# A delta-rule attention and FFN block: half of the small matmuls turned to other columns of the array, and a 64x64 block-diagonal state

## What is computed

```python
def step(S, inp):                      # per head: S is 32x32
    qt, kt, vt, bt = inp
    v_pred = einsum('bhk,bhkv->bhv', kt, S)
    delta = (vt - v_pred) * bt[..., None]
    S = S + kt[..., None] * delta[:, :, None, :]
    ot = einsum('bhk,bhkv->bhv', qt, S)
...
q = xn @ Wq;  k = xn @ Wk;  v = silu(xn @ Wv);  beta = sigmoid(xn @ Wb)
o = delta_rule(l2norm(q) * 32**-0.5, l2norm(k), v, beta)
o = o * rsqrt(mean(o*o) + eps) * o_norm_weight;   attn = o @ Wo
ffn = down(silu(gate(xn)) * up(xn))
return x + attn + ffn
```

## Time and profile before

| | |
|---|---|
| runs, median (lowest to highest) | 2339.17 us (2338.87 to 2341.85) |
| the profiled execution | 2343.81 us |
| its span, first to last instruction | 2342.1 us |
| PE, DVE, ACT busy | 2235.0, 1786.9, 857.9 us |
| mean granted TensorE clock | 0.993 of full |

### The profile page before, as it was taken

One profiled execution on the slowest core, in us unless ns is written; L12 is line 12 of the kernel. 1 busy time (PEld: TensorE's weight loads), 2 busy tenths in 40 slices (PEclk: granted clock), 3 DMA queues, 4 the chain that ended last, 5 costly groups with the idle time before them and its releaser, 6 DMA issues.

```text
span 2342.1 us, 89426 instructions
## 1 busy us (share of the span) xinstructions
PE 2235.0 (95%) x40464; PEld 1228.6 (52%) x40688; DVE 1786.9 (76%) x3167; ACT 857.9 (37%) x2077; POOL 265.7 (11%) x519
## 2 busy tenths in 40 slices
PE   2899999999999999999999999999999999999996
PEld 1455555555546555455555546555455555546553
DVE  8986968778686786968768696786968768697775
ACT  4652524325242342523325242342423325242341
POOL 2101010020100101011020100101011020100100
PEclk9899999999999999999999999999999999999998
DMA  7000111101111001111001111001111001111000
GB/s 256 20 7 17 37 21 38 17 7 38 21 37 22 24 16 21 37 22 38 12 12 38 21 37 22 15 26 21 37 21 38 12 12 38 21 37 22 12 10 20
DMA packets 89978, 68.96 MB, mean 29 GB/s; under 512 B 68480, under 2 KB 68480, under 8 KB 89600
## 3 DMA queue, kind: packets, MB, share of 16 engines
q1 hardware_dynamic: 88880, 63.20, 9.6%
q10 hardware_dynamic: 720, 0.03, 0.0%
HBM read 30.72 MB, written 16.78 MB: 20 GB/s over the span
## 4 chain that ended last, share of the span: by engine, by line
PE 93%; DVE 4%; issue 2%; DMA 1%; ACT 0%; SPq 0%
PE D L440 28%; PE T L355 22%; PE D L430 22%; PE D L506 14%; PE D L371 7%; DMA qt<-in_L_attn_Wq_dram 1%; DVE outer_v L1198 1%; DVE at L1205 1%; DVE amax L935 0%; DVE kq L925 0%; DVE wd L926 0%; DVE wgu L926 0%; DVE f_hi L925 0%; DVE f_lo L925 0%; DVE qt L1383 0%
## 5 line engine op out<-in xcount | busy, mean ns | idle before, releaser
L440 PE MATMUL D<-xt,wgu 128*128 128x512 f16 x3072 | 689.6, 381 | 8.2 <-ACT sg L720 6.4
L430 PE MATMUL D<-xt,w_hi 128*128 128x512 f16 x1664 | 489.1, 380 | 24.4 <-DVE w_lo L978 24.4
L440 PEld LDWEIGHTS D<-xt,wgu 128*128 128x128 f16 x3072 | 291.9, 98 | 357.0 <-ACT sg L720 6.9
L430 PE MATMUL D<-xt,w_lo 128*128 128x512 f16 x768 | 291.9, 380 | 0.0
L1205 DVE TENSOR_TENSOR at<-at,outer_v 128x62 f32<-128x62 f32 (+15 forms) x496 | 262.2, 529 | 11.8
L1198 DVE TENSOR_TENSOR outer_v<-mt,at 128x62 f32<-128x62 f32 (+15 forms) x496 | 260.9, 526 | 13.0
L430 PEld LDWEIGHTS D<-xt,w_hi 128*128 128x128 f16 x1664 | 159.0, 98 | 212.7 <-issue 26.2
L506 PE MATMUL D<-wd,f_hi 128*128 128x512 bf16 x656 | 248.7, 379 | 17.8 <-issue 17.8
L506 PE MATMUL D<-wd,f_lo 128*128 128x512 bf16 x656 | 248.8, 379 | 16.1 <-issue 15.3
L710 ACT ACTIVATE kpv<-kpv,rk 128x32 f32<-128x32 f32 x1024 | 231.1, 307 | 1.5
L772 ACT ACTIVATE qt<-T 128x256 f32<-128x256 f32 x128 | 49.0, 383 | 465.4 <-DVE outer_p L1341 465.4
(11 more groups left out here) (173 smaller groups left out, 2597.5 us busy)
## 6 DMA issues: line engine op xcount, KB each, us to landing
xs<-_attn_hidden_states_dram SPq DMA_DIRECT2D x32, 512.0 KB, 3.5
out_dram<-xs SPq DMA_DIRECT2D x32, 512.0 KB, 3.0
fuse<-in_L_ffn_gate_w_dram SPq DMA_DIRECT2D x2, 768.0 KB, 8.3
xs<-in_L_ffn_up_w_dram SPq DMA_DIRECT2D x2, 768.0 KB, 9.1
f_hi<-in_L_ffn_down_w_dram SPq DMA_DIRECT2D x2, 768.0 KB, 10.1
f_lo<-in_L_ffn_down_w_dram SPq DMA_DIRECT2D x2, 768.0 KB, 11.7
kpv<-in_L_attn_Wk_dram SPq DMA_DIRECT2D x1, 1024.0 KB, 11.0
qt<-in_L_attn_Wq_dram SPq DMA_DIRECT2D x1, 1024.0 KB, 13.0
```

What stands on the lines that cost most here:

```text
L430: last = nc.tensor.matmul(D[bank][:, :], w[:, k, cols], xp[:, k, :], start=n == 0, stop=n == len(products) - 1)
L440: last = nc.tensor.matmul(D[bank][:, :], wgu[:, n // 2, c:c + P], (xt_hi, xt_lo)[n % 2][:, n // 2, :], start=n == 0, stop=n == 2 * KT_ - 1)
```

## The change

**Turned layout.** The batches are no longer alike. For batch 1 everything that lies by tokens (kt, vt, pt, the solution tt, beta) has its 64-partition halves swapped, so its matmuls go from strip h of the inputs to strip h^2 of the output: off the diagonal of the array, into the other bank of a pair. In all small stages the calls of batch 0 and batch 1 now alternate, quad by quad; before, 8 quads (or 4 in the chain) of one batch followed each other.

**Block state.** `state` gets two 32x32 slots per strip, one zero, so two heads stand on the diagonal of a 64x64 block. The prediction uses `pairs`: two 64x64 matmuls in place of a quad of four 32x32, 16 in place of 32 a step. DVE updates the state in two masked operations (`of_pair` is 0 or 1 by partition).

**Output.** Q S and P (U - W S) now lie in columns of their own (128 columns per group m instead of 96). ACT copies Q S, DVE adds the other (`add_inner`), one step later.

**Turning.** Reads that turn batch 1 are split in three, one over 128 partitions and two over 64: K transposes, beta's sum, the U copies, the output copies. V goes through ACT first (Silu from PSUM to `sg`), then DVE transposes. `V_AT` moves. `gram(2m)` and `gram(2m+1)` become one call with one semaphore at its end, as do the two U and W calls of a group.

```diff
-V_AT = {0: 0, 2: 1, 7: 2, 12: 3}
+V_AT = {0: 0, 4: 1, 8: 2, 13: 3}
...
+            def pairs(out, lhs, rhs, turned):
+                for h in range(2):
+                    s = slice(64 * h, 64 * h + 64)
+                    to = slice(64 * (1 - h), 64 * (1 - h) + 64) if turned else s
+                    last = nc.tensor.matmul(out[to], lhs[s], rhs[s], start=True, stop=True)
...
                 for h in range(QUADS):
                     s = slice(32 * h, 32 * h + 32)
-                    last = nc.tensor.matmul(out[s], lhs[s], rhs[s], start=start, stop=True, skip_group_check=shared)
+                    to = slice(32 * (h ^ 2), 32 * (h ^ 2) + 32) if turned else s
+                    last = nc.tensor.matmul(out[to], lhs[s], rhs[s], start=True, stop=True)
...
-                            pe.wait_ge(u_ready, since(8, g - 3))
+                            pe.wait_ge(u_ready, since(8, 2 * m - 2))
...
-                        for b in range(BATCH):
-                            for m in range(MS):
+                        for m in range(MS):
+                            for b in range(BATCH):
                                 pc = m * BC + b * STEPS + c
-                                last = quads(T[2 * (c % 2) + b][:, 96 * m:96 * m + 64], state[:, b, m, :],
-                                             kq_flat[:, 64 * pc:64 * pc + 64], start=m == 0, shared=True)
+                                last = pairs(T[2 * (c % 2) + b][:, 128 * m:128 * m + 64], state[:, b, m, :, :].rearrange("p e d -> p (e d)"),
+                                             kq_flat[:, 64 * pc:64 * pc + 64], b == 1)
...
-                        nc.scalar.activation(vt[:, 8 * g:8 * g + 8, :],
-                                             T[g % 4][:, :].rearrange("p (n a d) -> p n a d", n=8, a=2)[:, :, 1, :],
-                                             ACT.Copy).then_inc(u_ready, 1)
+                        for to, src in parts_of(g % 2):
+                            last = nc.scalar.activation(vt[to, 8 * g:8 * g + 8, :], made[src, :, 1, :], ACT.Copy)
+                        last.then_inc(u_ready, 1)
...
-                        nc.vector.tensor_tensor(state[:, :, :, :], state[:, :, :, :], blocks(outer_p), ALU.add).then_inc(s_ready, 1)
+                        for e in range(2):
+                            half = state[:, :, :, e, :].rearrange("p b m d -> p (b m) d")
+                            ins = nc.vector.scalar_tensor_tensor(half, outer_p[:, 0:256].rearrange("p (n d) -> p n d", d=DH), of_pair[:, e:e + 1], half,
+                                                                 ALU.mult, ALU.add)
+                        ins.then_inc(s_ready, 1)
...
+                    def add_inner(c):
+                        dve.wait_ge(q_out, since(STEPS, c + 1))
+                        nc.vector.tensor_tensor(ot_v[:, :, c], ot_v[:, :, c], chain_banks(c)[:, :, :, 2, :], ALU.add).then_inc(o_ready, 1)
...
                         nc.vector.tensor_tensor(u, u, blocks(outer_v), ALU.subtract).then_inc(r_ready, 1)
+                        if c:
+                            add_inner(c - 1)
```

More of the change, by code:

```diff
@@ L529, in all_spans @@
                     pe.wait_ge(vk_ready, since(1, 1))
-                    for g in range(8):
-                        pe.wait_ge(tt_ready, since(2, g // 4 + 1))
-                        if g < 4:
+                    for m in range(MS):
+                        pe.wait_ge(tt_ready, since(2, m // 2 + 1))
+                        if m < 2:
                             pe.wait_ge(m_ready, since(2, 2))
@@ L702, in all_spans @@
                     for m in range(MS):
-                        act.wait_ge(v_raw, since(MS, m + 1))
-                        v_group = flat(vt)[:, m * TOK:(m + 1) * TOK]
-                        nc.scalar.activation(v_group, v_group, ACT.Silu, scale=w_inv[:, 2:3]).then_inc(v_ready, 1)
+                        full(("job", JOB_V[m]))
+                        if m >= 2:
+                            act.wait_ge(v_ready, since(MS, m - 1))
+                        for b in range(BATCH):
+                            tokens = slice(b * SPAN_B, (b + 1) * SPAN_B)
+                            for to, src in parts_of(b):
+                                last = nc.scalar.activation(sg[to, m % 2, tokens], D[bank_of(JOB_V[m])][src, tokens], ACT.Silu, scale=w_inv[src, 2:3])
+                        last.then_inc(v_raw, 1)
                     def values_by_k(n):
@@ L771, in all_spans @@
                         act.wait_ge(ds_read, since(STEPS, c + 1))
-                        nc.scalar.activation(ot_v[:, :, c], chain_banks(c)[:, :, :, 1, :], ACT.Copy).then_inc(o_ready, 1)
+                        for b in range(BATCH):
+                            for to, src in parts_of(b):
+                                last = nc.scalar.activation(ot_v[to, b, c], chain_banks(c)[src, b, :, 1, :], ACT.Copy)
+                        last.then_inc(q_out, 1)
             all_spans()
@@ L910, in one @@
                 dve.wait_ge(set_v, done[0])
+            for h in range(QUADS):
+                for e in range(2):
+                    one(nc.vector.memset(of_pair[32 * h:32 * h + 32, e:e + 1], float(h % 2 == e)))
             for b in range(BATCH):
@@ L1061, in k_to_tokens @@
                         dve.wait_ge(kwide_ready, since(MS, m + 1))
-                        nc.vector.transpose(kt[:, m * BC:(m + 1) * BC, :], kq[:, m * BC:(m + 1) * BC, 0, :]).then_inc(kt_ready, 1)
+                        for b in range(BATCH):
+                            of_b = slice(m * BC + b * STEPS, m * BC + (b + 1) * STEPS)
+                            for to, src in parts_of(b):
+                                last = nc.vector.transpose(kt[to, of_b, :], kq[src, of_b, 0, :])
+                        last.then_inc(kt_ready, 1)
                     def v_to_tokens(m):
-                        bank = full(JOB_V[m])
-                        nc.vector.transpose(group(vt, m), D[bank][:, :]).then_inc(v_raw, 1)
+                        dve.wait_ge(v_raw, since(MS, m + 1))
+                        nc.vector.transpose(group(vt, m), sg[:, m % 2, :]).then_inc(v_ready, 1)
                     def b_to_tokens():
@@ L1071, in b_to_tokens @@
                         dve.wait_ge(b_raw, since(1, 1))
-                        nc.vector.tensor_tensor(tb[:, :, :], bt[:, :, 0:MS].rearrange("p c m -> p m c"),
-                                                bt[:, :, MS:2 * MS].rearrange("p c m -> p m c"), ALU.add).then_inc(b_summed, 1)
+                        for b in range(BATCH):
+                            of_b = slice(b * STEPS, (b + 1) * STEPS)
+                            for to, src in parts_of(b):
+                                last = nc.vector.tensor_tensor(tb[to, :, of_b], bt[src, of_b, 0:MS].rearrange("p c m -> p m c"),
+                                                               bt[src, of_b, MS:2 * MS].rearrange("p c m -> p m c"), ALU.add)
+                        last.then_inc(b_summed, 1)
                     def beta_to_problems():
```

66 lines of the change are left out of this document (37 added, 29 removed).

## The result

| | before | changed |
|---|---|---|
| median | 2340.27 us (2338.87 to 2341.85, 4 runs) | 2286.34 us (2283.62 to 2288.38, 4 runs) |
| ratio | | 0.9769, 95% interval 0.9752 to 0.9786 |
| span of the profiled execution | 2342.1 us | 2286.6 us |

A forecast was written before the change was run, and what follows sets the result against it. PE, busy for 95% of the span, was taken as the bound. Per span 3.6 + 1.6 + 7.1 - 1.2 = 11.1 us, with first span and end -173 us: median 2339.2 becomes 2166 us, range 2145 to 2240.

The forecast's parts named there:

- projections and grams, quick span: Gram visits: alternating batches save half of each visit's rounds, 4 x 0.89 = 3.6 us a span.
- U and W: U and W stage: DVE's last read comes 1.9 us earlier, last U copy 0.3 longer; 1.6 us saved, ends 0.3 and 2.0.
- chain: Chain stage: 16 visits save 0.446 us each, 7.1 us a span, against 1.2 us lost to DVE's added work.
- opening and end: First span saves only 7.5 us, as DVE holds up PE before U and W; the last output add costs 1 us.
- I take half, because ... the issue rate leaves exactly the room: Small-tile visits: rounds of both batches share 56 ns, eight starts at 7 ns; saving between nothing and half, half taken.
- Chain on DVE: Chain: the second masked operation and `add_inner` use up DVE's slack, so PE waits; 1.2 us a span lost.
- Solve at nothing: Solve stage: DVE is ready about when the grams come, with 0.6 us of slack; costed at nothing.
- No overlap: Rival, 8%: the strip's input is the limit, rounds stay 56 ns; 2345 us, 0.25% above.
- Loads queue: Rival, 13%: two blocks on a strip load one after the other, so only 7.2 us a span is saved; 2227 us.
- strict order: Rival, 7%: matmuls start in program order, two passes cannot overlap on a block; 6.9 us a span saved, 2231 us.
- clock rival: Rival, 10%: PE's new 2 us idle stretch per span ahead of the chain lets the clock fall, costing 26; 2192 us.
- Switching costs: Rival, 7%: a quad changing the block on a strip pays some 25 ns, 6.7 us more a span; 2448 us.

The follow-up runs named there:

- reads together: The good kernel with DVE's last two reads of W one right behind the other, the second batch's statistics after both: 2233.04 us, ratio 0.9544.
- good kernel: The changed kernel plus already fulfilled PE waits, 221 in the first span and 14 in each later one, aligning spans to 256 instructions: 2251.48 us, ratio 0.9616.
- blocked kernel: The changed kernel with its turned layout but no alternation, all of batch 0's quads and pairs before batch 1's: 2341.93 us, ratio 1.0002.
- second cut kernel: The good kernel with gram and U and W visits cut into pieces of 32 matmuls, large ones between, last U and W visit whole: 2329.87 us.

## Why the prediction was wrong, step by step

Set against the forecast, the 15 periods and what lies around them. The stages are those of the two periods in the windows, the quick period is a mean:

| | forecast | measured |
|---|---|---|
| projections and grams, quick span | -3.6 us | -2.1 (31.66 to 29.58) |
| U and W | -1.6 | +0.2 (15.53 to 15.77) |
| chain | -5.9 | -3.5 (42.44 to 38.95); -3.8 by the medians |
| solve | 0 | 0.0 (50.82 both) |
| quick period | -11.1 | -6.0 (140.9, the mean of before, to 134.9, of the six quick ones) |
| 15 periods | -166.5 | -90 if all were quick, -53 as they are |
| opening and end | -6.5 | -2.8 |

Of the 118 us that are missing, 77 would be missing if all spans were quick, 37 are what the slow ones add, and 4 lie in the opening and at the end. The 37 are instructions that come late, 5 of them by the clock that falls behind a stop; aligning the borders gave 35 back. Of the 77, some 13 are also stops of this kind, since a quick span has nearly 1 us more of them than a span of before.

**The step that failed first** is "I take half, because ... the issue rate leaves exactly the room". The 7 ns came from four starts at the head of a visit, and I used it as a rate for 128. The head is quicker than what follows; the rate that holds on was nowhere in the trace of before, since a round of 56 ns asked for one matmul per 14 ns. In its place the runs showed 10.7 ns a matmul behind the first 32. Right was the mechanism: the blocks do work side by side. A pair visit gains 0.405 us of the 0.446 forecast: four of its matmuls start every 58 ns, one per 15 ns, which asks for less than the sustained rate. A quad visit of 64 gains 0.25, one of 128 gains 0.52 and 0.49 in place of 0.89 and 0.93. (Half of 32 rounds of 60 ns is 0.96 and not 0.93; it changes nothing, as the forecast there went by DVE.) By visits that is 2.1 us for grams and 5.2 for the chain, where 3.6 and 7.1 were forecast. The bounds I gave the saving, nothing and half, held it, but between the two stood no case of its own.

**The step that wasn't there**, put at nothing without a word, is the supply in pieces of 256. It has a row in the page of before, of the section on queues (packets, MB, share):

```profile
q8 instruction: 321, 5.26, 1.0%
```

Before also had three "issue" waits inside its visits, 0.9 us in all. I read neither as something that the change could move. The count of instructions was to be had: 5120 a span is a multiple of 256, 4594 is not. A visit of 256 instructions used to last 1.8 us and now would last 1.3, while PE goes on some 2.6 us after a packet's start.

**U and W** were forecast at 1.6 us for an earlier last read. The stage's visits did shrink, by less than forecast, and the gain ended on DVE: with the batches alternating, both tiles are full only at the visit's end, and the second read still stood behind 1.24 us of statistics. In the kernel before these stood there too, between the reads of the earlier trace rows, and covered the time in which the second tile was filled:

```profile
1281.59 1.24 DVE L894 BATCH_NORM_STATS2 stats<-xs 128x6 f32<-128x512 f32 x2
```

PE's wait ahead of the chain, forecast at 2 us, is 1.2 to 1.6, 1.3 on average. The run with the reads together got 18 us back for moving one line, so the term was there to be had, and the step that failed was to shift all of DVE's reads by what the visits save.

**Chain on DVE**: forecast 1.2 us of waits a span; the waits in the chain are 0.9 in the good kernel, so the size was about right, and the place was not. I had put them in steps 1 to 4, by DVE's added work; they are 0.63 us in step 4, where a masked operation meets POOL's addition, and 0.19 in step 6; 0.09 more are a wait for the subtraction in step 3. Without the second operation 1.45 us a span come back.

**Solve at nothing** held to 0.01 us in every quick span, and DVE's wait for the last gram fell from 3.82 to 1.00 us; I had said near zero. In spans 7 to 9 the stage is 1.7 us longer by the half clock behind the stop, and in span 12 it is 2.1 us longer, with a stop of 1.96 us in its projections.

**The rivals.** No overlap falls with the visits and with the blocked kernel, which is what it described, at 2342. Loads queue and strict order fall with the first eight starts in 47 ns and the next eight from 80 ns on: two quads with both their passes take two rounds of 56 ns and not 168, and 64-column pairs keep nearly the same pace, 58 ns. The clock rival had the wrong place: behind PE's new idle stretch ahead of the chain, 1.2 to 1.6 us, the clock stayed at 1.00. It did fall behind three stops in gram visits, which cost 5 us and not 26. In the second cut kernel, whose idle stretch there is 2.5 to 3.0 us, it fell as the rival says. Switching costs exist, 0.24 us for each change between large and small, and the change adds none; between blocks there are none to be seen. The true case was none of the five.

## What to carry to other kernels

A rate read from the first few instructions of a burst need not hold: here it held for 32 matmuls. Ask how many instructions the burst has, and whether anything before has held that pace to its end. Where a stage issues instructions faster than before, count them per loop and per 256, and move the borders with a few fulfilled waits before judging the change: here that alone spans 2251 to 2353 us. The best version (turned, aligned, reads together) is at 2233.04 us, 4.6% under the kernel before, of which the change as written had given 2.3.

## What the runs showed of the hardware

- PE's instructions come in packets of 16,384 bytes, 256 instructions. Behind the 335 stalls of over 0.5 us inside visits, in all runs together, PE goes on 2.1 to 3.0 us after the last packet's start and 1.2 to 1.7 after its end; the longest is 2.7 us from start to start. Placed badly, the borders cost over 6 us in a span of 135, the fallen clock included.
- Small float32 matmuls (64 columns, two blocks on a strip) start every 7.5 ns for the first 32 of a visit, then every 10.7 on average; with 32 columns it is 5 and then 8.3 ns. One block on a strip takes 56 ns a round.
- Behind stops of PE of 1.8 to 2.2 us in the changed kernel, and idle stretches of 2.5 to 3.0 in the second cut one, the granted clock was 0.50 for 3.41 us; behind 1.2 to 1.6 us ahead of the chain it stayed at 1.00. Not each long stop has it: the one of 2.03 us in span 10 doesn't.
- A change from 128x128 matmuls to 32x32 ones and back costs 0.24 us beside the matmuls themselves.
- DVE's masked operation on 128x256 float32 takes 0.48 us, and 0.85 on average where it overlaps an addition on POOL.
